# The last sample's tail: halves in another order on TensorE, two roots ahead of an output on GpSimd, two GELUs ahead of a norm on ScalarE

## The chip, the cores and the metric

One core of a Trainium2 chip runs the whole program in one launch. Its engines are TensorE (PE, matmuls; its weight loads are listed apart as PEld), VectorE (DVE), ScalarE (ACT), GpSimd (POOL) and SyncE (SP, which issues the DMAs). Each runs its own list of instructions in the order in which it is written and waits on semaphores. The metric is the device time of one launch in microseconds, the median of several runs.

## The reference

Four stages are applied to eight samples of 512 tokens with 256 features, all in float32. Only the last three touch the change.

```python
x = x + (ctx @ Wo + bo)                              # attention block
x = x + gelu2((ln(x) * g2 + beta2) @ W1 + b1) @ W2 + b2    # feed-forward "network"
# adapter 1 (domain expert), then rotation, then adapter 3 (the same with other weights):
hidden = gelu(x @ down_W.T + down_b)                 # 256 -> 64, exact GELU
hidden = hidden @ expert_W[idx].T + expert_b[idx] + domain_emb[idx]
x = hidden @ up_W.T + up_b + x                       # 64 -> 256, and the residual
x = (x - mu) * rsqrt(var + 1e-5) * ln_gamma + ln_beta
# rotation: pairs of features are turned by the sample's angles (theta, phi)
out = stack([x0*ct + x1*st, -x0*st + x1*ct, ...])
```

## The kernel before

The program has an attention part (to about 730 us) and a network part. In the network part a loop over samples j is software-pipelined: while sample j goes through the feed-forward network, sample j-1 is in adapter 1 (l = 0) and sample j-2 in adapter 3 (l = 1). Data lie mostly with features on the 128 partitions, as two feature halves c = 0, 1 (DC = 2) of 512 tokens. A layer norm needs tokens on the partitions, so TensorE transposes into PSUM banks, VectorE takes statistics, and GpSimd computes (variance + eps) ** -0.5, called a root here (`inverse_root`, `near_inverse_root`, `last_root`).

The loop ends before the last sample. The rest is written out by hand, engine by engine, for samples w = 5, y = 6 and z = 7 (the names `near_...` belong to sample 6, `end_...` and `last_...` to sample 7). The order of these calls at the end of each engine's block is the whole schedule: there is no planner. Sample 7 is cut in two token halves h = 0, 1 of 256 tokens (two tiles t of 128 each), so that engines overlap. Its steps, each with its line in the profile:

- `last_network` (DVE L1927) adds residual and bias to the second layer's result, once for each c and h, and counts `end_x2_done` in the order (h0,c0), (h1,c0), (h0,c1), (h1,c1).
- `last_down(l, h)` (PE L1630) multiplies by the down weights, summing over c; `last_hidden(l, h)` (ACT L2118) is the GELU on it.
- `last_residual(l, h)` (PE L1645) transposes the residual into PSUM by a matmul with the identity; `last_up(l, h)` (PE L1653) adds the up product on top.
- `last_statistics` (DVE L1948, L1934, L1936: statistics, aggregation, and variance + eps into `end_std`), `last_root` (POOL L2226), `last_normalise` (DVE L1954).
- `last_features` (PE L1664) transposes back, `last_features_out` (ACT L2124) copies to SBUF as `end_feat`, and `last_turned` (DVE L1962 tensor_scalar twice, then L1966 scalar_tensor_tensor twice) applies the rotation into `end_x4`.
- The same again with l = 1, and then `last_scale` (L1972) and `last_output` (L1980) on DVE, and two stores by SP (L1388).

Beside these steps the engines still finish samples 5 and 6. ScalarE normalises both (`normalise_w` L2131, `near_normalise` L2139), and GpSimd multiplies by gamma and adds beta for both: `output(w)` is `scale` (L2194) and `shift` (L2200), and sample 6 has `near_scale` (L2237) and `near_output` (L2243). Each of these four is one TENSOR_TENSOR of 128x1024 that reads and writes SBUF. `keep_busy` (L261) issues matmuls whose result nobody reads. `link` on DVE marks an instruction and waits for it, where the next one needs its result.

Of the kernel before, what the change touches and what calls it, by code (L numbers as in the profile page):

```python
# [1208 lines left out]
def network_block(nc, d, v, k, x1_dram):  # L1209
# [10 lines left out]
    with ExitStack() as ctx:  # L1220
# [3 lines left out]
        def sem(name):  # L1224
            return ctx.enter_context(nc.semaphore(name))
# [30 lines left out]
        def wait(eng, signal, j, n):  # L1256

            value = signal.at(j, n)
            if value > 0:
                eng.wait_ge(signal.sem, value)  # L1260
# [45 lines left out]
        end_res = x3[:, 0].rearrange("p c (u d) -> p (c u) d", d=D)  # L1306
        end_stats, end_mv = sb("end_stats", [P, 2, QT, 6]), sb("end_mv", [P, 2, QT, 2])
        end_std, end_rstd = sb("end_std", [P, 2, QT]), sb("end_rstd", [P, 2, QT])
        end_down, end_gelu, end_up0, end_up1, end_shifted, end_root, end_norm = (sem("end_" + n) for n in (
            "down", "gelu", "up0", "up1", "shifted", "root", "norm"))  # L1310
        end_x2_done, end_back, end_feats, end_x4_done, end_out, end_stored, end_step = (sem("end_" + n) for n in (
            "x2", "back", "feats", "x4", "out", "stored", "step"))
        END_A, END_B = (2, 0), (3, 1)
# [1 line left out]
        def end_tile(l, n):  # L1315

            h, t = divmod(n, ET)
            return bank[END_B[h]][:, t * D:(t + 1) * D] if l == 0 else bank[4 + n][:, 0:D]

        def cols(h):  # L1320

            return slice(h * EH, (h + 1) * EH)
# [71 lines left out]
        def _(pe):  # L1394
# [226 lines left out]
                        if t == QT - 1:  # L1621
                            last.then_inc(to_t[2].sem, 1)

            def last_down(l, h):
                for c in range(DC):
                    if l == 0:
                        pe.wait_ge(end_x2_done, 2 * c + h + 1)
                    elif c == 0:
                        pe.wait_ge(end_feats, DC * (h + 1))
                    last = pe.matmul(bank[END_A[h]][HALVES[l], 0:EH], k["down_w"][:, 0, c] if l == 0 else end_down_w[:, c],  # L1630
                                     (end_x2, end_feat)[l][:, c, cols(h)], start=(c == 0), stop=(c == DC - 1), tile_position=(0, A * l))
                last.then_inc(end_down, 1)

            def last_residual(l, h):

                if l == 0:
                    pe.wait_ge(end_x2_done, 2 * DC if h else DC + 1)
                elif h == 1:
                    wait(pe, norm_done[2], y, 1)
                for c in range(DC):  # L1640
                    if l == 1:
                        pe.wait_ge(end_x4_done, DC * h + c + 1)
                    for t in range(ET):
                        tok = h * EH + t * P
                        pe.matmul(end_tile(l, ET * h + t)[:, c * P:(c + 1) * P], (end_x2, end_x4)[l][:, c, tok:tok + P], ident[:],  # L1645
                                  start=(c == 0 and (l == 1 or t == 0)), stop=False, is_transpose=True, skip_group_check=True)

            def last_up(l, h):
                pe.wait_ge(end_gelu, nth(l, h))
# [45 lines left out]
            up_of_two()  # L1695
            for q in range(4, 8):
                second_layer(z, q)
            last_down(0, 0)
            last_residual(0, 0)
            last_down(0, 1)  # L1700
            last_up(0, 0)
            last_residual(0, 1)
            last_up(0, 1)
            wait(pe, norm_done[2], w, 1)
            keep_busy(pe, bank[5], w2h[:, 0], 4)
            last_features(0)
            last_features(1)
            last_down(1, 0)
            last_residual(1, 0)
            last_down(1, 1)  # L1710
            last_up(1, 0)
            last_residual(1, 1)
            last_up(1, 1)

        @block.vector
        def _(dve):
# [154 lines left out]
            def link(ins):  # L1871

                steps[0] += 1
                ins.then_inc(end_step, 1)
                dve.wait_ge(end_step, steps[0])
# [82 lines left out]
            def last_turned(h):  # L1958

                dve.wait_ge(end_feats, DC * (h + 1))  # L1960
                for c in range(DC):
                    last = dve.tensor_scalar(end_scaled[:, c, cols(h)], end_feat[:, c, cols(h)], turn[:, 0, c, z:z + 1],  # L1962
                                             turn_b[:, c, z:z + 1], ALU.mult, ALU.add)
                link(last)
                for c in range(DC):
                    dve.scalar_tensor_tensor(end_x4[:, c, cols(h)], end_feat[:, 1 - c, cols(h)], turn[:, 1, c, z:z + 1],  # L1966
                                             end_scaled[:, c, cols(h)], ALU.mult, ALU.add).then_inc(end_x4_done, 1)

# [54 lines left out]
        def _(act):  # L2023
# [91 lines left out]
            def last_hidden(l, h):  # L2115
                act.wait_ge(end_down, nth(l, h))
                rows = HALVES[l]
                act.activation(end_hid[rows, cols(h)], bank[END_A[h]][rows, 0:EH], ACT.Gelu, bias=end_down_b[rows, 0:1]  # L2118
                               ).then_inc(end_gelu, 1)

            def last_features_out(h):
                act.wait_ge(end_back, h + 1)
                for c in range(DC):
                    act.copy(end_feat[:, c, cols(h)], bank[END_A[h]][:, c * EH:(c + 1) * EH]).then_inc(end_feats, 1)  # L2124

            def normalise_w():

                act.wait_ge(near_shift, 1)
                wait(act, scaled, w - 1, 1)
                for t in range(QT):  # L2130
                    last = act.activation(features(xh[:, 2, t], 2), halves(bank[4 + t // 2][:, (t % 2) * D:(t % 2 + 1) * D]), ACT.Identity,  # L2131
                                          bias=std[:, 2, t:t + 1], scale=rstd[:, 2, t:t + 1])
                last.then_inc(norm_done[2].sem, 1)

            def near_normalise():

                act.wait_ge(near_shift, 2)
                for t in range(QT):
# [17 lines left out]
            gelu(z, 7)  # L2156
            hidden_of_two()
            normalise_w()
            near_normalise()
            last_hidden(0, 0)  # L2160
            last_hidden(0, 1)
            last_features_out(0)
            last_features_out(1)
            last_hidden(1, 0)
            last_hidden(1, 1)

        @block.gpsimd
        def _(pool):
# [84 lines left out]
            output(w - 1)  # L2253
            inverse_root(w, 2)
            near_inverse_root(1)
            output(w)
            near_scale()
            last_root(0, 0)
            last_root(0, 1)
            near_output()  # L2260
            last_root(1, 0)
            last_root(1, 1)
# [92 lines left out]
```

## Time and profile before

| | us |
|---|---|
| median of 3 runs | 1001.78 (1001.27 to 1002.12) |
| the profiled execution, as device time | 1005.43 |
| its span in the trace | 1003.6 |
| PE / DVE / ACT / POOL busy in it | 941.1 / 753.2 / 689.6 / 699.7 |
| mean granted TensorE clock | 0.986 of full speed |
| core's engines from 979 to 1003.6: PE / DVE / ACT / POOL busy | 14.72 / 15.46 / 5.74 / 12.25 of 24.60 |

The profiled execution is 3.65 us longer than the median run, and 1.8 us of it lie outside the span. Nearly all of the program is bound by TensorE (941.1 of 1003.6 us), but the change touches only what comes after the last sample's second layer, from about 979 us on. There TensorE is busy for 60% of the time and the engines wait for one another. So the views to read are the chain that ended last, and the timeline of each engine over the last 25 us. In a timeline, instructions of one line that follow one another are merged: x4 with 1.90 us are four of them, and a start plus the time is the end of the last. An instruction's time includes what it waited for after it was started, for instance for the way to memory; the idle time in brackets comes before the start.

### The profile page before, as it was taken

To read this page: it belongs to the slowest core of one execution; us is meant where nothing else is said; L and a number is where in the kernel's file an instruction comes from. 1 tells how busy PE (TensorE), PEld (TensorE's weight loads), DVE (VectorE), ACT (ScalarE), POOL (GpSimd) and SP (SyncE) were. 2 spreads that over 40 slices of the span, in tenths; PEclk is the share of its full clock that TensorE was granted. 3 is DMA by queue.
4 is the path that set the end of the run, shared out by engine and by line. 5 is a ranking of instruction groups with operands and counts; after the bars stand their busy time and mean duration, and the time that the engine had idled before them with its cause. 6 is when DMAs were issued, how large, how long until landed. Compare 5 with 4: busy or idle time off the path is not lost. (4 is left out here: it accounts for less than half of the span.)

```text
span 1003.6 us, 20024 instructions
## 1 busy us (share of the span) xinstructions
PE 941.1 (94%) x5838; PEld 619.2 (62%) x5838; DVE 753.2 (75%) x2002; ACT 689.6 (69%) x1124; POOL 699.7 (70%) x540
## 2 busy tenths in 40 slices
PE   5879999999998999999999899989999999999996
PEld 4646656655655665665565566555477777777573
DVE  7787878789869787887878888788444765668466
ACT  3377888798788789778879787978644444444332
POOL 2468788788869778877876987876554545557465
PEclk9889999999999999999999999999999999999998
DMA  8977996996897799599689879966111110111101
GB/s 271 300 294 265 371 359 229 342 389 239 297 389 284 278 361 357 196 335 384 237 292 372 333 242 342 372 250 232 64 64 43 42 43 22 42 64 42 43 22 63
DMA packets 127533, 229.96 MB, mean 229 GB/s; under 512 B 6512, under 2 KB 53872, under 8 KB 123632
## 3 DMA queue, kind: packets, MB, share of 16 engines
q1 hardware_dynamic: 127472, 229.26, 63.0%
q8 instruction: 25, 0.41, 0.2%
q14 instruction: 36, 0.29, 0.1%
HBM read 187.30 MB, written 41.94 MB: 228 GB/s over the span
## 5 line engine op out<-in xcount | busy, mean ns | idle before, releaser
L935 ACT ACTIVATE prob<-prob,nmax 128x512 f32<-128x512 f32 x512 | 356.9, 729 | 60.5 <-DVE nmax L760 57.7
L760 DVE CUSTOM_DVE_ANT_0 prob<-s_bank,big 128x512 f32<-128x512 f32 x512 | 339.4, 686 | 70.1 <-POOL big L1099 31.2
L1099 POOL TENSOR_TENSOR big<-big,mterm_early 128x2048 f32<-128x2048 f32 (+2 forms) x88 | 305.2, 3484 | 72.4 <-DMA big<-in_fside_Bx16xSxS 63.0
L591 PEld LDWEIGHTS t_bank<-ident,prob 128*128 128x128 f32 x2048 | 239.8, 141 | 167.9 <-issue 53.5
L591 PE MATMUL t_bank<-ident,prob 128*128 128x128 f32 x2048 | 318.4, 278 | 15.6 <-ACT prob L935 6.7
L942 ACT COPY pt<-t_bank 128x512 f32<-128x512 f32 x312 | 181.4, 584 | 58.0 <-PE t_bank L591 56.4
L579 PE MATMUL s_bank<-stack_k,stack_q 128*128 128x512 bf16 x512 | 196.5, 384 | 1.9 <-DVE nmax L760 1.6
L769 DVE COPY pt<-t_bank 128x512 f32<-128x512 f32 x200 | 137.5, 688 | 40.9 <-PE t_bank L591 40.6
L605 PE MATMUL o_bank<-pt,val 128*32 128x512 f32 x1024 | 122.9, 598 | 1.2 <-ACT pt L942 0.7
L2173 POOL TENSOR_TENSOR gl<-big,gh 128x512 fp32r<-128x512 f32 x64 | 83.1, 1306 | 49.4 <-DVE gh L1723 49.4
L2032 ACT ACTIVATE big<-bank,late 128x512 f32<-128x512 f32 x62 | 42.7, 690 | 72.6 <-PE bank L1438 69.0
L1099 POOL TENSOR_TENSOR big<-big,mterm_late 128x1024 f32<-128x1024 f32 (+1 forms) x16 | 50.0, 3123 | 31.7 <-DMA big<-in_fside_Bx16xSxS 31.7
L579 PEld LDWEIGHTS s_bank<-stack_k,stack_q 128*128 128x128 bf16 x512 | 50.2, 98 | 25.9 <-DVE nmax L760 12.5
L605 PEld LDWEIGHTS o_bank<-pt,val 128*32 128x32 f32 x1024 | 26.9, 109 | 59.4 <-issue 55.7
L2178 POOL TENSOR_TENSOR xtl<-xt,xth 128x512 fp32r<-128x512 f32 x14 | 17.7, 1281 | 58.0 <-ACT xt L2058 58.0
L581 PE MATMUL s_bank<-mterm_early,ident_bf 128*128 128x512 bf16 x152 | 58.0, 382 | 0.0
L1786 DVE SCALAR_TENSOR_TENSOR big<-bank,up_b,x 128x512 f32<-128x512 f32 x22 | 15.5, 745 | 53.8 <-PE bank L1512 53.8
L635 PE MATMUL spare<-xth,w_parts 128*128 128x512 f32 x128 | 52.5, 428 | 0.7 <-DVE xtl L807 0.7
L1438 PE MATMUL bank<-xth,w1h 128*128 128x512 f32 x124 | 51.6, 416 | 1.7 <-PEq L289 1.0
L1456 PE MATMUL bank<-gh,w2h 128*128 128x512 f32 x128 | 52.3, 409 | 0.0
L1456 PE MATMUL bank<-gh,w2l 128*128 128x512 f32 x128 | 50.2, 392 | 0.0
L1723 DVE CAST gh<-big 128x512 fp32r<-128x512 f32 x64 | 38.3, 610 | 14.6 <-ACT big L2032 14.3
(245 smaller groups left out, 1464.9 us busy)
## 6 DMA issues: line engine op xcount, KB each, us to landing
big<-in_fside_Bx16xSxS SPq DMA_DIRECT2D x128, 1024.0 KB, 8.0
pieces_dram<-pieces SPq DMA_DIRECT2D x64, 384.0 KB, 7.2
stack_q<-pieces_dram SPq DMA_DIRECT2D x15, 1024.0 KB, 8.1
stack_k<-pieces_dram SPq DMA_DIRECT2D x15, 1024.0 KB, 9.4
pieces_dram<-pieces SPq DMA_DIRECT2D x32, 256.0 KB, 7.4
xin<-in_x SPq DMA_DIRECT2D x8, 512.0 KB, 8.8
x_dram<-x SPq DMA_DIRECT2D x8, 512.0 KB, 2.6
x1r<-x_dram SPq DMA_DIRECT2D x8, 512.0 KB, 4.4
```

Source lines behind the costliest of these rows:

```text
L579: last = pe.matmul(bank, stack_q[:, h, t * P:(t + 1) * P], stack_k[:, h, :], start=True, stop=not by_pe)
L581: last = pe.matmul(bank, ident_bf[:], mterm[:, t, :], start=False, stop=True)
L591: last = pe.transpose(t_bank[n % 2][:, c * P:(c + 1) * P], prob[:, n % NT, c * P:(c + 1) * P], ident[:])
L605: last = pe.matmul(o_bank[VW * j:VW * (j + 1), :], val[:, c, G * g + j, :], pt[:, pt_slot(G * g + j), c, :], start=(c == 0), stop=(c == QT ...
L635: last = pe.matmul(spare[n % 2][:, :], wx[name][:, part, i * P:(i + 1) * P], x[:, part, :], start=(part == m == 0), stop=(part == 1 and m ...
L760: dve.tensor_tensor_reduce(out=prob[:, n % NT, :], in0=s_bank[n % 3][:, :], in1=bias[:, h % NB, t, :], scale=-1.0, scalar=3e38, op0=ALU.ad ...
L769: dve.tensor_copy(pt[:, pt_slot(h), :, t * P:(t + 1) * P], t_bank[n % 2][:, :].rearrange("p (c q) -> p c q", c=QT)).then_inc(evac[1].sem, 1)
L935: act.activation(tile, tile, ACT.Exp, bias=nmax[:, n % NT:n % NT + 1], scale=-1.0).then_inc(exped.sem, 1)
L942: act.copy(pt[:, pt_slot(h), :, t * P:(t + 1) * P], t_bank[n % 2][:, :].rearrange("p (c q) -> p c q", c=QT)).then_inc(evac[0].sem, 1)
L1099: pool.tensor_tensor(bias[:, h % NB, tiles], bias[:, h % NB, tiles], mterm[:, tiles], ALU.add).then_inc(masked.sem, 1)
L1456: last = pe.matmul(bank[c][:, :], w[:, f, c * P:(c + 1) * P], gx[:, f, :], start=(m == 0), stop=(m == len(parts) - 1))
L2173: pool.tensor_tensor(gl[:, f], g[:, f % NGT], gh[:, f], ALU.subtract).then_inc(gl_done.sem, 1)
```

## The change

On TensorE, `last_down` and `last_residual` are cut by feature half c. For l = 0 the parts with c = 0 now come ahead of those with c = 1. For l = 1 the two down products of a half stay together and the residual follows. The discarded matmuls of `keep_busy` ahead of `last_features(0)` go from 4 to 6, and 3 more stand between `last_features(0)` and `last_features(1)`. On ScalarE the two GELUs of sample 7's adapter 1 come ahead of sample 6's norm, and a new step `last_scaled(h)` makes one of the two products of the rotation (c = 1) that VectorE made before. On GpSimd, sample 5's `scale` is followed by sample 7's first two roots, and then by `shift` and `near_scale`.

```diff
-            def last_down(l, h):
-                for c in range(DC):
-                    if l == 0:
-                        pe.wait_ge(end_x2_done, 2 * c + h + 1)
-                    elif c == 0:
-                        pe.wait_ge(end_feats, DC * (h + 1))
...
-            def last_residual(l, h):
-
+            def last_down(l, h, c):
                 if l == 0:
-                    pe.wait_ge(end_x2_done, 2 * DC if h else DC + 1)
-                elif h == 1:
-                    wait(pe, norm_done[2], y, 1)
...
+                    pe.wait_ge(end_x2_done, 2 * c + h + 1)
+                elif c == 0:
+                    pe.wait_ge(end_feats, DC * (h + 1))
...
+            def last_residual(l, h, c):
+
+                if l == 0:
+                    pe.wait_ge(end_x2_done, 2 * c + h + 1 if h == 0 else 2 * DC)
+                else:
+                    pe.wait_ge(end_x4_done, DC * h + c + 1)
+                    if h == 1:
+                        wait(pe, norm_done[2], y, 1)
...
-            last_down(0, 0)
-            last_residual(0, 0)
-            last_down(0, 1)
+            last_down(0, 0, 0)
+            last_residual(0, 0, 0)
+            last_down(0, 1, 0)
+            last_down(0, 0, 1)
+            last_down(0, 1, 1)
+            last_residual(0, 0, 1)
             last_up(0, 0)
-            last_residual(0, 1)
+            last_residual(0, 1, 0)
+            last_residual(0, 1, 1)
             last_up(0, 1)
             wait(pe, norm_done[2], w, 1)
-            keep_busy(pe, bank[5], w2h[:, 0], 4)
+            keep_busy(pe, bank[5], w2h[:, 0], 6)
             last_features(0)
+            keep_busy(pe, bank[5], w2h[:, 0], 3)
             last_features(1)
...
             def last_turned(h):
                 dve.wait_ge(end_feats, DC * (h + 1))
-                for c in range(DC):
-                    last = dve.tensor_scalar(end_scaled[:, c, cols(h)], end_feat[:, c, cols(h)], turn[:, 0, c, z:z + 1],
-                                             turn_b[:, c, z:z + 1], ALU.mult, ALU.add)
-                link(last)
+                link(dve.tensor_scalar(end_scaled[:, 0, cols(h)], end_feat[:, 0, cols(h)], turn[:, 0, 0, z:z + 1],
+                                       turn_b[:, 0, z:z + 1], ALU.mult, ALU.add))
                 for c in range(DC):
+                    if c == 1:
+                        dve.wait_ge(end_scaled_done, h + 1)
                     dve.scalar_tensor_tensor(end_x4[:, c, cols(h)], end_feat[:, 1 - c, cols(h)], turn[:, 1, c, z:z + 1],
                                              end_scaled[:, c, cols(h)], ALU.mult, ALU.add).then_inc(end_x4_done, 1)
...
+            def last_scaled(h):
+                act.wait_ge(end_feats, DC * (h + 1))
+                act.activation(end_scaled[:, 1, cols(h)], end_feat[:, 1, cols(h)], ACT.Identity, bias=turn_b[:, 1, z:z + 1],
+                               scale=turn[:, 0, 1, z:z + 1]).then_inc(end_scaled_done, 1)
...
             normalise_w()
-            near_normalise()
             last_hidden(0, 0)
             last_hidden(0, 1)
+            near_normalise()
             last_features_out(0)
+            last_scaled(0)
             last_features_out(1)
             last_hidden(1, 0)
+            last_scaled(1)
             last_hidden(1, 1)
...
-            output(w)
-            near_scale()
+            scale(w)
             last_root(0, 0)
             last_root(0, 1)
+            shift(w)
+            near_scale()
             near_output()
```

GpSimd's last instructions before, from sample 5's gamma product on (`res` belongs to sample 5, `xt` to sample 6, `end_rstd` are sample 7's roots):

```order
L2194 TENSOR_TENSOR res<-xh,late 128x1024 [waits stored,norm_done2]
L2200 TENSOR_TENSOR res<-res,late 128x1024 [waits scaled]
L2237 TENSOR_TENSOR xt<-xh,late 128x1024 [waits norm_done2]
L2226 TENSOR_TENSOR end_rstd<-end_std,minus_half 128x2 [waits end_shifted] x2
L2243 TENSOR_TENSOR xt<-xt,late 128x1024 [waits scaled]
L2226 TENSOR_TENSOR end_rstd<-end_std,minus_half 128x2 [waits end_shifted] x2
```

and the same place now:

```order
L2210 TENSOR_TENSOR res<-xh,late 128x1024 [waits stored,norm_done2]
L2242 TENSOR_TENSOR end_rstd<-end_std,minus_half 128x2 [waits end_shifted] x2
L2216 TENSOR_TENSOR res<-res,late 128x1024 [waits scaled]
L2253 TENSOR_TENSOR xt<-xh,late 128x1024 [waits norm_done2]
L2259 TENSOR_TENSOR xt<-xt,late 128x1024 [waits scaled]
L2242 TENSOR_TENSOR end_rstd<-end_std,minus_half 128x2 [waits end_shifted] x2
```

The first two roots have moved up past two of the 128x1024 products, and three of those now stand in one row behind them.

VectorE's rotation of sample 7 before, both token halves (`big` here is `end_feat`'s partner `end_scaled` and `end_x4`):

```order
L1962 TENSOR_SCALAR big<-big,turn,turn_b 128x256 [waits end_feats]
L1962 TENSOR_SCALAR big<-big,turn,turn_b 128x256
L1966 SCALAR_TENSOR_TENSOR big<-big,turn 128x256 [waits end_step]
L1966 SCALAR_TENSOR_TENSOR big<-big,turn 128x256
L1962 TENSOR_SCALAR big<-big,turn,turn_b 128x256 [waits end_feats]
L1962 TENSOR_SCALAR big<-big,turn,turn_b 128x256
L1966 SCALAR_TENSOR_TENSOR big<-big,turn 128x256 [waits end_step]
L1966 SCALAR_TENSOR_TENSOR big<-big,turn 128x256
```

and now:

```order
L1969 TENSOR_SCALAR big<-big,turn,turn_b 128x256 [waits end_feats]
L1974 SCALAR_TENSOR_TENSOR big<-big,turn 128x256 [waits end_step]
L1974 SCALAR_TENSOR_TENSOR big<-big,turn 128x256 [waits end_scaled]
L1969 TENSOR_SCALAR big<-big,turn,turn_b 128x256 [waits end_feats]
L1974 SCALAR_TENSOR_TENSOR big<-big,turn 128x256 [waits end_step]
L1974 SCALAR_TENSOR_TENSOR big<-big,turn 128x256 [waits end_scaled]
```

Of each half's four instructions three are left, and the third has a wait for ScalarE.

## Rows read from the trace of the kernel before

**Rows 1.** Chain that ended last: start us, us, engine, tile, line

```profile
979.96 2.38 POOL res L2194
...
984.75 2.31 POOL xt L2237
...
990.84 1.90 PE bank L1630 x4
```

**Rows 2.** GpSimd's timeline: start us, us, engine, line, operation, xcount, [idle before]

```profile
987.02 1.37 POOL L2226 TENSOR_TENSOR end_rstd<-end_std,minus_half 128x2 f32<-128x2 f32 x2
988.37 2.35 POOL L2243 TENSOR_TENSOR xt<-xt,late 128x1024 f32<-128x1024 f32 x1
...
998.61 0.86 POOL L2226 TENSOR_TENSOR end_rstd<-end_std,minus_half 128x2 f32<-128x2 f32 x1 [1.35 <-DVE end_std L1936]
```

**Rows 3.** VectorE's timeline from 983 us

```profile
983.26 0.76 DVE L1948 BATCH_NORM_STATS2 end_stats<-bank 128x6 f32<-128x256 f32 x2 [3.06 <-PE bank L1653]
...
985.98 1.10 DVE L1936 TENSOR_SCALAR end_std<-end_mv 128x2 f32<-128x2 f32 x1
987.76 1.90 DVE L1954 TENSOR_SCALAR xh<-bank,end_mv,end_rstd 128x256 f32<-128x256 f32 x4 [0.68 <-POOL end_rstd L2226]
990.28 0.92 DVE L1962 TENSOR_SCALAR big<-big,turn,turn_b 128x256 f32<-128x256 f32 x2 [0.62 <-ACT big L2124]
991.23 0.88 DVE L1966 SCALAR_TENSOR_TENSOR big<-big,turn 128x256 f32<-128x256 f32 x2
...
995.12 0.86 DVE L1948 BATCH_NORM_STATS2 end_stats<-bank 128x6 f32<-128x256 f32 x2 [1.44 <-PE bank L1653]
```

**Rows 4.** Line L1936 in the whole trace: count, ns min/median/max, first and last start

```profile
L1936 DVE TENSOR_SCALAR end_std<-end_mv x4: 169/304/1101, 984.3 to 998.4; 128x2 f32<-128x2 f32 x4
```

**Rows 5.** Stretches: us, PE, PEld, DVE, ACT, POOL busy (xcount), granted clock, DMA share, GB/s

```profile
985.50:988.80 3.30, 0.03 (x1) 0.00 (x0) 2.56 (x7) 0.00 (x0) 3.30 (x4) 1.00 0.47 159
...
989.70:992.70 3.00, 2.99 (x9) 1.51 (x9) 2.39 (x6) 1.19 (x4) 1.02 (x1) 0.50 0.35 118
```

**Rows 6.** TensorE's timeline from 979 us

```profile
979.21 1.29 PE L1630 MATMUL bank<-end_x,late 128*64 128x256 f32 x4
980.43 0.65 PE L1645 MATMUL bank<-ident,end_x 128*128 128x128 f32 x4
...
982.09 1.13 PE L1653 MATMUL bank<-uw,end_hid 64*128 64x256 f32 x4
...
984.79 0.74 PE L261 MATMUL bank<-w2h 128*128 128x256 f32 x4
988.81 0.75 PE L1664 MATMUL bank<-ident,xh 128*128 128x128 f32 x4 [3.28 <-DVE xh L1954]
...
990.77 1.97 PE L1630 MATMUL bank<-big,end_down_w 128*64 128x256 f32 x4
...
993.37 1.08 PE L1630 MATMUL bank<-big,end_down_w 128*64 128x256 f32 x4
994.38 1.13 PE L1653 MATMUL bank<-uw,end_hid 64*128 64x256 f32 x4
```

**Rows 7.** ScalarE's timeline from 979 us

```profile
979.75 1.98 ACT L2139 ACTIVATE xh<-bank,near_std,near_rstd 128x256 f32<-128x256 f32 x4
...
989.60 0.65 ACT L2124 COPY big<-bank 128x256 f32<-128x256 f32 x2 [6.99 <-PE bank L1664]
```

**Rows 8.** Line L799 from 57 to 65 us: count, ns min/median/max

```profile
L799 DVE TENSOR_SCALAR xin<-xin,mv,rstd x4: 777/779/3486, 58.8 to 63.6; 128x256 f32<-128x256 f32 x4
```

**Rows 9.** GpSimd's timeline beside Rows 8

```profile
58.03 4.07 POOL L1099 TENSOR_TENSOR big<-big,mterm_early 128x2048 f32<-128x2048 f32 x1 [2.08 <-DMA big<-in_fside_Bx16xSxS]
62.19 1.32 POOL L1085 TENSOR_SCALAR mterm_late<-mraw 128x512 bf16<-128x512 uint8 x2
```

**Rows 10.** Line L884 in the whole trace: count, ns min/median/max

```profile
L884 DVE TENSOR_TENSOR rest<-proj,pieces x2: 693/1057/1421, 25.4 to 28.7; 128x512 f32<-128x512 f32 x2
```

**Rows 11.** GpSimd's timeline beside the first of Rows 10

```profile
25.08 1.23 POOL L1154 TENSOR_SCALAR xres<-xt 128x1024 f32<-128x1024 f32 x1
```

More of the change, by code:

```diff
@@ L1308, in network_block @@
         end_std, end_rstd = sb("end_std", [P, 2, QT]), sb("end_rstd", [P, 2, QT])
-        end_down, end_gelu, end_up0, end_up1, end_shifted, end_root, end_norm = (sem("end_" + n) for n in (
-            "down", "gelu", "up0", "up1", "shifted", "root", "norm"))
+        end_down, end_gelu, end_up0, end_up1, end_shifted, end_root, end_norm, end_scaled_done = (sem("end_" + n) for n in (
+            "down", "gelu", "up0", "up1", "shifted", "root", "norm", "scaled"))
         end_x2_done, end_back, end_feats, end_x4_done, end_out, end_stored, end_step = (sem("end_" + n) for n in (
@@ L1622, in up_of_two @@
                             last.then_inc(to_t[2].sem, 1)
-            def last_down(l, h):
-                for c in range(DC):
-                    if l == 0:
-                        pe.wait_ge(end_x2_done, 2 * c + h + 1)
-                    elif c == 0:
-                        pe.wait_ge(end_feats, DC * (h + 1))
-                    last = pe.matmul(bank[END_A[h]][HALVES[l], 0:EH], k["down_w"][:, 0, c] if l == 0 else end_down_w[:, c],
-                                     (end_x2, end_feat)[l][:, c, cols(h)], start=(c == 0), stop=(c == DC - 1), tile_position=(0, A * l))
-                last.then_inc(end_down, 1)
@@ L1634, in last_residual @@
-            def last_residual(l, h):
-                if l == 0:
-                    pe.wait_ge(end_x2_done, 2 * DC if h else DC + 1)
-                elif h == 1:
-                    wait(pe, norm_done[2], y, 1)
-                for c in range(DC):
[L1641 to L1646, printed above, removed]
+            def last_down(l, h, c):
+                if l == 0:
+                    pe.wait_ge(end_x2_done, 2 * c + h + 1)
+                elif c == 0:
+                    pe.wait_ge(end_feats, DC * (h + 1))
+                last = pe.matmul(bank[END_A[h]][HALVES[l], 0:EH], k["down_w"][:, 0, c] if l == 0 else end_down_w[:, c],
+                                 (end_x2, end_feat)[l][:, c, cols(h)], start=(c == 0), stop=(c == DC - 1), tile_position=(0, A * l))
+                if c == DC - 1:
+                    last.then_inc(end_down, 1)
@@ new lines, in last_residual @@
+            def last_residual(l, h, c):
[5 more added lines that the diff above has]
+                        wait(pe, norm_done[2], y, 1)
+                for t in range(ET):
+                    tok = h * EH + t * P
+                    pe.matmul(end_tile(l, ET * h + t)[:, c * P:(c + 1) * P], (end_x2, end_x4)[l][:, c, tok:tok + P], ident[:],
+                              start=(c == 0 and (l == 1 or t == 0)), stop=False, is_transpose=True, skip_group_check=True)
@@ L1697, in _ @@
                 second_layer(z, q)
-            last_down(0, 0)
-            last_residual(0, 0)
-            last_down(0, 1)
+            last_down(0, 0, 0)
[4 more added lines that the diff above has]
+            last_residual(0, 0, 1)
             last_up(0, 0)
-            last_residual(0, 1)
+            last_residual(0, 1, 0)
+            last_residual(0, 1, 1)
             last_up(0, 1)
             wait(pe, norm_done[2], w, 1)
-            keep_busy(pe, bank[5], w2h[:, 0], 4)
+            keep_busy(pe, bank[5], w2h[:, 0], 6)
             last_features(0)
+            keep_busy(pe, bank[5], w2h[:, 0], 3)
             last_features(1)
-            last_down(1, 0)
-            last_residual(1, 0)
-            last_down(1, 1)
+            last_down(1, 0, 0)
+            last_down(1, 0, 1)
+            last_residual(1, 0, 0)
+            last_residual(1, 0, 1)
+            last_down(1, 1, 0)
+            last_down(1, 1, 1)
             last_up(1, 0)
-            last_residual(1, 1)
+            last_residual(1, 1, 0)
+            last_residual(1, 1, 1)
             last_up(1, 1)
@@ L1960, in last_turned @@
                 dve.wait_ge(end_feats, DC * (h + 1))
+                link(dve.tensor_scalar(end_scaled[:, 0, cols(h)], end_feat[:, 0, cols(h)], turn[:, 0, 0, z:z + 1],
+                                       turn_b[:, 0, z:z + 1], ALU.mult, ALU.add))
                 for c in range(DC):
-                    last = dve.tensor_scalar(end_scaled[:, c, cols(h)], end_feat[:, c, cols(h)], turn[:, 0, c, z:z + 1],
-                                             turn_b[:, c, z:z + 1], ALU.mult, ALU.add)
-                link(last)
-                for c in range(DC):
+                    if c == 1:
+                        dve.wait_ge(end_scaled_done, h + 1)
                     dve.scalar_tensor_tensor(end_x4[:, c, cols(h)], end_feat[:, 1 - c, cols(h)], turn[:, 1, c, z:z + 1],
```

## The prediction

> **What bounds the kernel now.** I read the chain that ended last first, then each engine's timeline behind 979 us, then the clock. From 980 to 988.4 us the chain lies on GpSimd: samples 5 and 6's products of 128x1024, 2.3 to 2.4 us each, run one behind the other [rows 1], and sample 7's two roots come only at 987.02, two in 1.37 us [rows 2]. VectorE is held up as well: the 128x2 instruction that prepares the second root lasts from 985.98 for 1.10 us, to the end of GpSimd's product of 984.75, where 0.17 would do [rows 1, 3, 4]. Sample 7's normalise starts at 987.76. TensorE has nothing to do meanwhile: 0.03 us of 3.30 are busy [rows 5]. It comes back at 988.81, and soon has half of its clock (0.50 from 989.70 to 992.70, its 1.2 GHz level) [rows 5, 6]. The down product of half 0 therefore takes 1.97 us and not 1.08, and is in the chain [rows 1, 6]. From the statistics at 995.12 on, VectorE works through to the end.
>
> **The change, part by part.**
>
> *TensorE's new order in front.* Up (0,0) starts 2.88 us after 979.21 [rows 6]. Two down products at 1.01 (993.37 to 994.38) and a residual of four transposes at 0.65 make 2.7, without the wait for c = 1 that there was between the two down instructions: up (0,0) starts near 981.9; I take 0.15 earlier. Its GELU must be ready: the second down part of h = 0 ends near 981.2, and the GELU takes 0.5, as one of the four norm instructions of 256 columns does (1.98 for four) [rows 7], so 981.7. Before, that GELU stood behind sample 6's norm, which ended at 981.73. So ScalarE's swap is worth nothing beyond that 0.15. ScalarE idles for a microsecond and sample 6's norm ends near 984.2; GpSimd wants it much later.
>
> *GpSimd's roots.* Both halves' statistics move forward by the same 0.15 [rows 3]; GpSimd is idle from 982.34 [rows 1], so no 128x2 instruction is held up. The first variance is there at 984.3 - 0.15 + 0.17 = 984.3, the second at 985.98 - 0.15 + 0.17 = 986.0 [rows 3, 4]. Root 0 is long done, so normalise of half 0 starts at 986.0; root 1 runs from 986.07 to 986.77 (0.69 each [rows 2]); half 1 is normalised by 987.75 (0.95 each half), not 989.66: **1.9 us gained**.
>
> *The additional idle matmuls.* 0.185 us each (4 in 0.74) [rows 6]. Six end at 985.8, so TensorE's idle time shrinks to 1.1 us and I take the full clock for the features and for down (1,0). The three between the features cost 0.3 us; VectorE, below, hides them. down (1,0) ends near 989.7.
>
> *What is now beside the rotation.* This is the dear part. GpSimd's three products come from 986.77 on, 2.35 each [rows 2]: to 989.1, 991.5 and 993.9. VectorE's rotation falls right beside them. The copies for it end 1.45 us after the transposes' start (988.81 to 989.60, and 0.65) [rows 6, 7]; the transposes start behind half 0's normalise, at 986.95, so the copies end at 988.4. Before, only its first instruction met GpSimd: the pair of L1962 took 0.92 from 990.28, with GpSimd's last product until 990.72, and the two of L1966 ran free, 0.88 [rows 2, 3].
>
> What happens when both engines have a row of such instructions? The first of four L799 takes 3.49 us, to the end of GpSimd's product, and the three behind it take 0.78 each, though nothing but GpSimd's train of L1085 stands against them: VectorE and GpSimd take turns, one instruction each [rows 8, 9]. L884, which has two inputs in SBUF as L1966 has, takes 1.42 us and not 0.69 behind a GpSimd instruction of 1.23 [rows 10, 11]. So I let every instruction of the rotation wait for one product:
>
> - tensor_scalar (h0, c0): issued at 988.4, runs when the first product ends, done at 989.2. A link follows, and GpSimd's second product is in before the next instruction.
> - scalar_tensor_tensor (h0, c0): behind the second product (which VectorE pushed back a little, to 991.5): done at 991.9.
> - scalar_tensor_tensor (h0, c1): behind the third, 991.8 to 994.15: done at **994.5**.
> - h1: 0.4, then 0.45 twice, free: done at 995.7.
>
> Before, (h0, c1) was done at 992.11 [rows 3]. ScalarE's new product (0.5 us) is ready long before and saves nothing here. TensorE now waits from 989.7 to 994.5 with 0.3 us of work in it, an idle time longer than the one that halved the clock before [rows 5]; so it comes back at half clock. Then: half a residual 0.5 (0.65 for a whole one at full clock, less overlap), down (1,1) 1.9 (1.97 less its overlap with the next), first tile of up (1,0) 0.75 (994.38 to 995.12). Statistics (1,0) start at 994.5 + 0.05 + 0.5 + 1.9 + 0.75 = 997.7 instead of 995.12. VectorE's end behind it is as before (no big product is left then, and up (1,1) keeps ahead). **Sum: +2.6 us**: 1.9 gained at the norm, 4.5 lost behind it. Made against the profiled span it gives 1006.2 (1008.0 as its device time); the median runs are 3.65 us under that, and I carry the difference over as it is: 1001.78 + 2.6 = 1004.4.
>
> Bounds of what no row shows. A scalar_tensor_tensor with two SBUF inputs beside a GpSimd product: at best unhindered, 0.44 [rows 3], at worst one product each, 2.35; I take the second, for that of L884 is nearest [rows 10]. The only hint at L1966's own kind is the root of 998.61, which took 0.86 beside L1980 and not 0.69 [rows 2]. ScalarE's Identity product of 128x256: 0.33 to 0.5 [rows 7], off the path. The stores of samples 5 and 6 are issued 4.4 and 3.5 us later, at 989 and 994.2, and have left the queue before sample 7's. TensorE's end at half clock: nothing up to 2 us, if up (1,1) falls in it as well.
>
> The Trainium skill says it too ("SBUF — State Buffer", Who interferes with whom): a VectorE instruction contends with a GpSimd instruction that reads SBUF if it has two SBUF inputs, and the loser is blocked for the whole instruction. By that rule the time is the +2.6 above; by the trace of L1966 alone [rows 3], where it met no product, it would be the second rival's. The trace agrees for tensor_tensor, 1.42 against 0.69 us [rows 10]; no row shows it for scalar_tensor_tensor held up by GpSimd.
>
> **Rivals.**
>
> 1. *The clock stays up.* The same waits, but half a residual, down (1,1) and up cost 0.3 + 1.0 + 0.74: statistics at 996.6, **+1.5 us, 1003.3**. For it: 5 more idle matmuls. Against: the long wait comes behind all of them.
> 2. *Only tensor_scalar waits.* Then the two behind it follow at once, x4 of h0 is whole at 990.2; the tensor_scalar of h1 waits for the second product (991.7), statistics (1,0) start at 992.6, the variance meets the end of the third product for nothing. 995.12 - 992.6 = **2.5 us faster, 999.3**. For it: the 0.88 of L1966. Against: L884 [rows 10]. This is the case on the other side; it decides at whether scalar_tensor_tensor is held by a product.
> 3. *VectorE keeps its turn.* Both scalar_tensor_tensor and the tensor_scalar of h1 go together between the second and third product; only the last two wait, to 995.7, where statistics begin: **+0.6 us, 1002.4**. Against: L799 [rows 8].
> 4. *No turn is lost, but the gain is*: something else, as the norm of half 1 or the stores, gives the 1.9 back. **0, 1001.8**.
>
> **How the numbers follow.** About 2.0 us, 0.2%, is what a measurement of this kernel can tell from no change. Forecast (its own range 1003.3 to 1005.4): 0.48, of it 0.40 slower by over 0.2% and 0.08 within. Rival 1: 0.12 (0.03 slower, 0.09 within). Rival 2: 0.25 (0.21 faster, 0.04 within). Rival 3: 0.10 and rival 4: 0.05, within. That makes faster 0.21, same 0.36, slower 0.43. The range of 8 in 10 has to take in most of rival 2: 999.0 to 1005.2.
>
> **What would show it.** Right: roots at about 984.4 and 986.1; normalise from 986.0; then three GpSimd products in a row with a VectorE instruction of about 2.4 us ending behind each of the second and third; TensorE's longest idle time before residual (1,0) and down (1,1), with granted clock 0.5 there; statistics (1,0) near 997.7. Wrong: L1974 at 0.48 beside a product (rival 2), or both L1974 behind one product (rival 3); the clock at 1.0 in down (1,1) (rival 1); or a first normalise not before 987, which would upset every step.

## The result, and the profile after

The changed kernel takes 1003.78 us (median of 22 runs, 1001.90 to 1008.25), the kernel before 1000.78 us (22 runs beside them). The ratio is 1.004 with a 95% interval of 1.003 to 1.005: 3 to 5 us slower, where 2.6 us were forecast, and 1003.78 is inside the forecast's own range.

The two profiled executions can't be compared by their spans (1003.6 before, 1002.5 after), since the part ahead of the change, the same program in both, took 5.5 us less in the second. So every kernel below is compared by its **tail**: from VectorE's first `last_network` instruction with c = 1 (979.32 us before, 973.84 after) to the end of its last output (1001.01, and 999.02 + 0.88 = 999.90 after). Times with a plus sign are counted from that first instruction.

| | norm starts | x4 (h0, c1) done | statistics (1,0) start | tail |
|---|---|---|---|---|
| before | +8.44 | +12.79 | +15.80 | 21.70 |
| after, forecast | +6.7 | +15.2 | +18.4 | 24.3 |
| after, measured | +6.61 | +14.93 | +18.76 | 26.06 |

The chain that ended last, in the kernel after (start us, us, engine, tile, line):

```profile
980.54 0.91 DVE xh L1962 x2
...
982.96 0.86 DVE big L1969
...
983.85 4.94 DVE big L1974 x2
...
988.83 0.69 PE bank L1644 x2
989.51 1.90 PE bank L1629 x4
991.41 2.00 PE bank L1652 x4
993.42 1.04 PE bank L1644 x4
994.46 2.02 PE bank L1652 x4
```

GpSimd is no longer in it, but VectorE's two scalar_tensor_tensor of the rotation are, with 4.94 us. GpSimd's timeline, which answers to [rows 2]:

```profile
978.98 0.70 POOL L2242 TENSOR_TENSOR end_rstd<-end_std,minus_half 128x2 f32<-128x2 f32 x1 [2.10 <-DVE end_std L1944]
980.62 0.70 POOL L2242 TENSOR_TENSOR end_rstd<-end_std,minus_half 128x2 f32<-128x2 f32 x1 [0.95 <-DVE end_std L1944]
981.29 2.38 POOL L2216 TENSOR_TENSOR res<-res,late 128x1024 f32<-128x1024 f32 x1
983.62 2.39 POOL L2253 TENSOR_TENSOR xt<-xh,late 128x1024 f32<-128x1024 f32 x1
986.09 2.40 POOL L2259 TENSOR_TENSOR xt<-xt,late 128x1024 f32<-128x1024 f32 x1
```

and VectorE's, which answers to [rows 3]:

```profile
982.96 0.85 DVE L1969 TENSOR_SCALAR big<-big,turn,turn_b 128x256 f32<-128x256 f32 x1 [0.61 <-ACT big L2132]
983.85 4.92 DVE L1974 SCALAR_TENSOR_TENSOR big<-big,turn 128x256 f32<-128x256 f32 x2
988.70 0.40 DVE L1969 TENSOR_SCALAR big<-big,turn,turn_b 128x256 f32<-128x256 f32 x1
989.13 0.88 DVE L1974 SCALAR_TENSOR_TENSOR big<-big,turn 128x256 f32<-128x256 f32 x2
992.60 0.43 DVE L1956 BATCH_NORM_STATS2 end_stats<-bank 128x6 f32<-128x256 f32 x1 [2.59 <-PE bank L1652]
```

Read the two side by side. The tensor_scalar of 982.96 ends at 983.81, when the product of 981.29 is over; two scalar_tensor_tensor take 4.92 us and end at 988.77, when the products of 983.62 and 986.09 are both over; the same two take 0.88 us in the next half, where GpSimd is idle. The waits are inside the instructions' times: no idle time stands ahead of them. The four of L1974 by themselves (count, ns min/median/max), where 477 is one that waits for nothing:

```profile
L1974 DVE SCALAR_TENSOR_TENSOR big<-big,turn x4: 477/1464/2556, 983.8 to 989.5; 128x256 f32<-128x256 f32 x4
```

TensorE's timeline, which answers to [rows 6]:

```profile
979.19 0.98 PE L261 MATMUL bank<-w2h 128*128 128x256 f32 x6
981.50 0.75 PE L1663 MATMUL bank<-ident,xh 128*128 128x128 f32 x4 [1.33 <-DVE xh L1962]
...
983.08 1.08 PE L1629 MATMUL bank<-big,end_down_w 128*64 128x256 f32 x4
986.35 0.44 PE L1644 MATMUL bank<-ident,big 128*128 128x128 f32 x2 [2.19 <-DVE big L1974]
988.83 0.69 PE L1644 MATMUL bank<-ident,big 128*128 128x128 f32 x2 [2.04 <-DVE big L1974]
989.45 1.97 PE L1629 MATMUL bank<-big,end_down_w 128*64 128x256 f32 x4
991.34 2.07 PE L1652 MATMUL bank<-uw,end_hid 64*128 64x256 f32 x4
```

and stretches of it (us, PE, PEld, DVE, ACT, POOL busy, granted clock, DMA share, GB/s), which answer to [rows 5]:

```profile
983.00:986.30 3.30, 1.16 (x6) 0.47 (x4) 3.26 (x3) 2.16 (x5) 3.22 (x3) 1.00 0.47 159
986.30:988.83 2.53, 0.44 (x3) 0.20 (x3) 2.53 (x2) 0.00 (x0) 2.19 (x1) 0.59 0.00 0
988.83:996.40 7.57, 7.57 (x18) 4.08 (x18) 3.63 (x11) 0.47 (x1) 0.71 (x1) 0.50 0.20 69
```

Down (1,0), which had half the clock before, has all of it now (1.08 us). After the two waits the clock is at 0.50, the 1.2 GHz level, for everything that TensorE still has to do: down (1,1) 1.97, both up products 2.07 each where 1.13 would do.

### The profile page after: what moved, and what is told of

The parts are those of the page before. It is cut to its first block and busy times, and to the rows that moved or that the text cites. A ratio compares the mean times of both kernels' runs of the same rounds, so it can differ in the third digit from the quotient of the medians.

```text
span 1002.5 us, 19955 instructions
## 1 busy us (share of the span) xinstructions
PE 933.0 (93%) x5763; PEld 616.2 (61%) x5843; DVE 754.7 (75%) x2000; ACT 689.9 (69%) x1126; POOL 699.9 (70%) x540
## 5 line engine op out<-in xcount | busy, mean ns | idle before, releaser
L579 PE MATMUL s_bank<-stack_k,stack_q 128*128 128x512 bf16 x432 | 165.3, 383 | 2.1 <-DVE nmax L760 1.8
```

The lines of the kernel that those rows point to most:

```text
L579: last = pe.matmul(bank, stack_q[:, h, t * P:(t + 1) * P], stack_k[:, h, :], start=True, stop=not by_pe)
```

## The experiments

Each kernel was profiled once and, but for one, timed in rounds with the kernel before, whose median was 999.67 us beside e1 to e4, 1000.53 beside e5 to e8 and 1002.45 beside e9 and e10. All tails are of the one profiled execution. The ratios are those of the record, and not quotients of the medians.

| | edit | tail | ratio to before (95%) |
|---|---|---|---|
| before | | 21.70 | |
| after | | 26.06 | 1.003 to 1.005 |
| e1 | before, with the new GpSimd order alone | 26.53 | 1.0047 to 1.0088 |
| e2 | after, without the new GpSimd order | 21.79 | 1.0003 to 1.0023 |
| e3 | after, rotation reads PSUM | 19.14 | 0.9969 to 0.9993 |
| e4 | after, idle matmuls in the waits | 23.08 | 1.0021 to 1.0049 |
| e5 | after, only scalar_tensor_tensor reads PSUM | 19.18 | 0.9957 to 0.9995 |
| e6 | after, products in quarters | 20.42 | 0.9955 to 0.9989 |
| e7 | after, one product less | 20.89 | not timed |
| e8 | e3 with three more edits | 19.61 | 0.9940 to 0.9975 |
| e9 | e3 with 14 idle matmuls | 19.13 | 0.9948 to 0.9996 |
| e10 | e8 with 14 idle matmuls, ScalarE reordered | 18.63 | 0.9950 to 0.9988 |

**e1, the new GpSimd order alone.**

```diff
-            output(w)
-            near_scale()
+            scale(w)
             last_root(0, 0)
             last_root(0, 1)
+            shift(w)
+            near_scale()
             near_output()
```

> The kernel before, with GpSimd's new order alone (scale of sample 5, sample 7's two roots, then three 128x1024 products); TensorE, ScalarE and VectorE as before. The tail is counted from VectorE's first last_network instruction with c = 1 to the end of its last output: 21.70 us in the profile of before, 26.06 of after. My theory (each VectorE instruction of the rotation waits for one product): the norm starts 1.8 us earlier, at +6.6 to +6.8, the rotation's first three instructions end behind one product each and x4 of (h0, c1) is done near +15.3, where it was +12.79; TensorE comes back at half clock; tail 25 to 26.5 us, time +3 to +4 us against before. Rival (the loss lies in TensorE's new order, the nine idle matmuls or ScalarE's work): this kernel keeps the gain of the roots and is 1.5 to 2 us faster than before, tail near 20.

Measured: a tail of 26.53 us, 1004.38 us against 999.67, ratio 1.0067 (1.0047 to 1.0088), which is more than the 3 to 4 us that I expected. The norm starts at +6.74, x4 (h0, c1) is done at +15.37. The whole loss is in this one edit. VectorE's timeline of it, with two tensor_scalar per half as before:

```profile
981.67 3.18 DVE L1962 TENSOR_SCALAR big<-big,turn,turn_b 128x256 f32<-128x256 f32 x2 [0.61 <-ACT big L2124]
984.89 2.91 DVE L1966 SCALAR_TENSOR_TENSOR big<-big,turn 128x256 f32<-128x256 f32 x2
```

The products there run from 980.00, 982.32 and 984.78. The first tensor_scalar waits for the first, the second, though no semaphore stands between the two, for the second, and the first scalar_tensor_tensor for the third: three turns in another split. The fourth instruction is free.

**e2, everything but the new GpSimd order.**

```diff
-            scale(w)
+            output(w)
+            near_scale()
             last_root(0, 0)
             last_root(0, 1)
-            shift(w)
-            near_scale()
             near_output()
```

> The changed kernel with GpSimd's order as it was before (sample 5's output, sample 6's gamma product, then sample 7's roots, then one product). My theory: all the loss is the roots' move, so this one has none of it; the norm starts at +8.3, one product meets only the first tensor_scalar of the rotation, and the six idle matmuls leave TensorE idle for 2.8 us, so the clock may or may not fall: tail 20.5 to 22 us, time -1.3 to +0.3 us against before. Rival (the loss is in the rest of the change): +3 us, tail near 25.

Measured: a tail of 21.79 us, 1000.26 us against 999.67, ratio 1.0013 (1.0003 to 1.0023), so 0.3 to 2.3 us slower, at or above the upper end of what I expected. The rival is out: the rest of the change costs at most 0.2%, and it brings nothing. The profile says why: with the norm at +8.48 TensorE is idle for 3.21 us ahead of the features, more idle matmuls or not, and down (1,0) again takes 1.97 us. ScalarE's new product also has a price that I had missed, since it stands behind a GELU that waits for that slow down product:

```profile
988.88 0.48 DVE L1974 SCALAR_TENSOR_TENSOR big<-big,turn 128x256 f32<-128x256 f32 x1 [1.39 <-ACT big L2137]
```

**e3, the rotation reads the features from PSUM.** The features lie in the PSUM bank from which ScalarE copies them, so VectorE can take them there; the down product, which would overwrite that bank, goes to another, and ScalarE's GELU reads it there (that line is left out here).

```diff
-link(dve.tensor_scalar(end_scaled[:, 0, cols(h)], end_feat[:, 0, cols(h)],
+link(dve.tensor_scalar(end_scaled[:, 0, cols(h)], bank[END_A[h]][:, 0:EH],
...
-dve.scalar_tensor_tensor(end_x4[:, c, cols(h)], end_feat[:, 1 - c, cols(h)],
+dve.scalar_tensor_tensor(end_x4[:, c, cols(h)], bank[END_A[h]][:, (1 - c) * EH:(2 - c) * EH],
...
-pe.matmul(bank[END_A[h]][HALVES[l], 0:EH],
+pe.matmul(bank[(END_A, END_B)[l][h]][HALVES[l], 0:EH],
```

> The changed kernel, with VectorE's rotation reading the features from their PSUM bank and not from SBUF (so scalar_tensor_tensor has one SBUF input, and tensor_scalar none); down (1,h) writes its product to the bank of sample 7's first norm, which is free by then. GpSimd's order stays the new one. My theory (what waits is an instruction with two SBUF inputs, or a tensor_scalar from SBUF to SBUF): the three products no longer hold the rotation, L1974's takes 0.9 us for two and not 4.92, x4 of (h0, c1) is done near +10, TensorE stays at the full clock, tail 18 to 19.5 us, time -2 to -3.5 us against before. Rival (VectorE is slowed by GpSimd's products whatever it reads, for instance by its write to SBUF): L1974 still takes 4 us or more, time +2 to +4.

Measured: a tail of 19.14 us, 996.97 us against 999.67, ratio 0.9981. Its timelines of VectorE and of GpSimd:

```profile
981.34 0.54 DVE L1969 TENSOR_SCALAR big<-bank,turn,turn_b 128x256 f32<-128x256 f32 x1 [0.61 <-ACT big L2132]
981.92 0.88 DVE L1974 SCALAR_TENSOR_TENSOR big<-bank,turn,big 128x256 f32<-128x256 f32 x2
```

```profile
979.66 2.38 POOL L2216 TENSOR_TENSOR res<-res,late 128x1024 f32<-128x1024 f32 x1
981.99 2.37 POOL L2253 TENSOR_TENSOR xt<-xh,late 128x1024 f32<-128x1024 f32 x1
```

The same three products run at the same place (the third from 984.43), and the rotation runs through them at its own speed; the tensor_scalar takes 0.54 us from PSUM where it takes 0.40 from SBUF. It is what VectorE reads that makes it wait, and not GpSimd's being busy. Without the waits the clock stays at 1.00 to the end of TensorE's work. The tail is 2.56 us shorter than before's, and 1.83 us of that are the earlier norm. No run reads from PSUM with the old GpSimd order, so what the new order alone is worth is not shown.

**e4, the clock alone.**

```diff
             last_down(1, 0, 1)
+            wait(pe, norm_done[2], y, 1)
+            keep_busy(pe, bank[7], w2h[:, 0], 11)
             last_residual(1, 0, 0)
+            keep_busy(pe, bank[7], w2h[:, 0], 12)
             last_residual(1, 0, 1)
```

> The changed kernel with idle matmuls in TensorE's two long waits: 11 ahead of residual (1,0,0) and 12 ahead of residual (1,0,1), 0.16 us each. The waits of the rotation stay as they are. My theory (the clock is a loss of its own behind the waits): x4 of (h0, c1) is done at +14.9 as in after, granted clock 1.00 in down (1,1) and both up products, statistics (1,0) at +17.0 and not +18.76, tail 22.8 to 24 us, so 2 to 3 us faster than after and 0.5 to 1.5 slower than before. Rival (the clock costs little, the statistics wait for VectorE and ScalarE anyway): within 0.5 us of after.

The wait that is added, for sample 6's norm, was over long before (at 979.17). Measured: a tail of 23.08 us, 1002.00 us against 999.67, ratio 1.0035 (1.0021 to 1.0049). VectorE's waits are the same (x4 (h0, c1) at +15.02), TensorE's timeline and clock are not:

```profile
989.94 1.08 PE L1629 MATMUL bank<-big,end_down_w 128*64 128x256 f32 x4
990.95 1.13 PE L1652 MATMUL bank<-uw,end_hid 64*128 64x256 f32 x4
```

```profile
985.00:994.00 9.00, 7.33 (x43) 5.20 (x42) 7.93 (x13) 1.39 (x3) 4.86 (x3) 1.00 0.35 118
```

So of the 4.36 us by which the tail of after is longer than before's, the half clock is 26.06 - 23.08 = 2.98 us, and the rest is 23.08 - 21.70 = 1.38 us. That rest is a difference: from the norm's start to x4 (h0, c1) e4 takes 8.41 us and before 4.35, so the waits cost 4.06 more than before; the norm gives 1.83 of it back, and 0.84 comes back between x4 and the statistics (2.17 us and not 3.01), where before's TensorE was still in its slow down (1,0).

This holds for the two profiled executions. The timed runs don't confirm its size: I expected e4 to be 0.5 to 1.5 us slower than before and 2 to 3 faster than after, and it is 2.1 to 4.9 slower than before, where after is 3 to 5 slower. The profile rules out why the rival thought that the clock costs little (the statistics start at +17.19 and not +18.76), but how much of the 2.98 us there is in a usual execution stays open.

**e5, only scalar_tensor_tensor reads PSUM.** As e3 without its first edit: tensor_scalar reads `end_feat` again.

> As e3_from_psum, but only the scalar_tensor_tensor of the rotation reads PSUM; its tensor_scalar again goes from SBUF to SBUF. This is the state that my second rival assumed, so it also tests that rival's arithmetic. My theory: the first tensor_scalar lasts to the end of the first product (0.85 us as in after), the two L1974 behind it take 0.9 together; the tensor_scalar of h1 waits for the second product and takes some 1.5 to 2 us; x4 of (h0, c1) near +10.9, tail 19 to 20 us, time -1.5 to -2.8 us against before. Rival (scalar_tensor_tensor waits for its write, or for the tensor_scalar's result, rather than for a second SBUF input): L1974 over 2 us for two, tail over 22.

Measured: a tail of 19.18 us, ratio 0.9976. VectorE:

```profile
983.03 0.85 DVE L1969 TENSOR_SCALAR big<-big,turn,turn_b 128x256 f32<-128x256 f32 x1 [0.61 <-ACT big L2132]
983.91 0.88 DVE L1974 SCALAR_TENSOR_TENSOR big<-bank,turn,big 128x256 f32<-128x256 f32 x2
984.70 1.53 DVE L1969 TENSOR_SCALAR big<-big,turn,turn_b 128x256 f32<-128x256 f32 x1
```

Each tensor_scalar waits for a product, each scalar_tensor_tensor with one input in SBUF goes free. The down product writes to the other bank here as in e3, and the tensor_scalar waits all the same, so that move is not what frees VectorE. It is the state that the second rival of the prediction took for the kernel after, and its 2.5 us under before are met in the tail (21.70 - 19.18 = 2.52), with 0.5 to 4.3 us in the times.

**e6, the products in quarters.** Each of the three products is four instructions of 128x256.

```diff
+            def quarters(dst, src, other, op, done):
+                for t in range(QT):
+                    last = pool.tensor_tensor(dst[:, t], src[:, t], other, op)
+                last.then_inc(done.sem, 1)
```

> The changed kernel with GpSimd's three products behind the roots cut in four instructions of 128x256 each; nothing else differs. My theory (a VectorE instruction waits for the one GpSimd instruction that is running, and then has its turn): each wait falls from 2.4 to at most 0.6 us, the rotation of h0 ends near +10.5 to +11.5 where it was +14.93, TensorE keeps the full clock; GpSimd's row takes 7.2 to 9 us in all. Tail 19.5 to 21.5 us, time -0.5 to -2.5 us against before. Rival (VectorE waits until GpSimd's row is done, whatever its pieces): L1974 as long as in after, tail near 26.

Measured: a tail of 20.42 us, ratio 0.9972 (0.9955 to 0.9989), though the medians, 1000.09 and 1000.53 us, differ by only 0.44. Here are VectorE's line and the first two products of GpSimd's, count and ns min/median/max:

```profile
L1974 DVE SCALAR_TENSOR_TENSOR big<-big,turn x4: 829/885/942, 986.9 to 990.1; 128x256 f32<-128x256 f32 x4
```

```profile
L2221 POOL TENSOR_TENSOR res<-res,late x4: 725/729/730, 984.0 to 986.0; 128x256 f32<-128x256 f32 x4
L2221 POOL TENSOR_TENSOR xt<-xh,late x4: 773/838/907, 986.7 to 989.2; 128x256 f32<-128x256 f32 x4
```

No wait is longer than half a microsecond now (0.94 - 0.48). VectorE waits for the one instruction that is running, and then has its turn; x4 (h0, c1) is done at +12.12, later than my +10.5 to +11.5. The clock fell in this profile, and the rotation starts at +9.50 where it starts at +9.12 in after. That explains 0.38 us of the miss; the rest is that three instructions in a row each wait nearly half a microsecond.

**e7, one product less.** Sample 6's last product (its beta) is left out, with a root of 128x4 in its place.

```diff
             near_scale()
-            near_output()
+            wait(pool, scaled, y, 1)
+            pool.tensor_tensor(near_rstd[:, 0], near_std[:, 0], minus_half[:], ALU.pow).then_inc(out_made.sem, 1)
             last_root(1, 0)
```

> The changed kernel without sample 6's last product (its beta is not added; a root of 128x4 stands in its place), so two products and not three are in the row. My theory (one turn each): the second L1974 no longer waits; the pair takes 2.4 to 3 us and not 4.92, x4 of (h0, c1) is done near +12.6 to +13.6, 1.3 to 2.3 us earlier; the clock may still fall after 983. Rival (the pair waits for GpSimd to be idle and then runs): the same time, as the row is shorter by 2.35; what tells them apart is the end of the first L1974, which stays at +12.4 by mine.

Measured: a tail of 20.89 us (its one execution took 1000.27 us). The first scalar_tensor_tensor is done at +12.44 as in after (+12.45), the second at +12.84 and not +14.93: one turn less, 2.09 us less. The pair's row:

```profile
984.89 2.84 DVE L1974 SCALAR_TENSOR_TENSOR big<-big,turn 128x256 f32<-128x256 f32 x2
```

**e8, a better version.** To e3: no idle matmuls between the features, up (1,0) ahead of down (1,1), and variance + eps of adapter 3 on ScalarE (in e3 VectorE's took 0.67 us, to the end of the third product, where 0.17 would do).

```diff
             last_features(0)
-            keep_busy(pe, bank[5], w2h[:, 0], 3)
...
+            last_up(1, 0)
             last_down(1, 1, 0)
             last_down(1, 1, 1)
-            last_up(1, 0)
...
+            def last_shift(h):
+                act.wait_ge(end_meas, h + 1)
+                tiles = slice(ET * h, ET * (h + 1))
+                act.activation(end_std[:, 1, tiles], end_mv[:, 1, tiles, 1], ACT.Identity, bias=eps[:, 0:1]).then_inc(end_shifted, 1)
```

> From e3_from_psum, three more edits for a better version: no idle matmuls between the features; sample 7's up (1,0) ahead of down (1,1) on TensorE; and variance + eps of adapter 3 computed by ScalarE (Identity with a bias) and not by VectorE, so that no 128x2 tensor_scalar waits for the third product. My theory: statistics (1,0) start at +11.6 to +12 and not +12.74, the norm's chain on VectorE is 0.2 to 0.7 shorter, tail 17.5 to 18.5 us against 19.14 in e3, time -3 to -4.5 us against before. Rival (the chain moves to GpSimd's root (1,0) behind the third product, or to ScalarE): tail 18.8 to 19.3.

Measured: 997.75 us against 1000.53, ratio 0.9958 (0.9940 to 0.9975), but the tail is 19.61 us, longer than e3's: my 17.5 to 18.5 is missed. The profiled execution, 1003.26 us, was the longest of its 12. In it TensorE has a gap of 1.33 us ahead of the features and its clock falls in down (1,0) behind them (1.00 from 986.80 to 988.40, 0.50 from 989.00 to 992.00), and x4 of (h1, c1) waited 0.60 us for ScalarE:

```profile
986.86 0.75 PE L1664 MATMUL bank<-ident,xh 128*128 128x128 f32 x4 [1.33 <-DVE xh L1966]
...
988.44 1.74 PE L1630 MATMUL bank<-big,end_down_w 128*64 128x256 f32 x4
```

**e9, the gap filled.** e3 with `keep_busy(..., 14)` for 6.

> As e3_from_psum, with 14 and not 6 idle matmuls ahead of the first features, so that TensorE's gap of 1.33 us before them is filled; the 3 between the features stay. In the profiles of after, e3, e4 and e5 the clock stayed up behind this gap, in those of e6, e7 and e8 it fell, with the same TensorE program to this point. My theory (it falls in some executions and costs about 1 us there): tail 19.1 us as in e3, no fall between the gap and down (1,1); median 0 to 0.8 us faster than e3's, which was 0.9981 of before, so 0.9970 to 0.9980. Rival (14 end too late and push the features back, or the gap never mattered): 0.9980 to 0.9990.

Measured: a tail of 19.13 us, ratio 0.9972 (0.9948 to 0.9996). The tail is e3's to 0.01 us, so 14 do no harm; whether they help, the timing can't tell (e3's interval, 0.9969 to 0.9993, overlaps). Inconclusive.

**e10, e8 with both mended.** 14 idle matmuls, and `last_scaled(1)` ahead of `last_hidden(1, 0)`.

> As e8_best, with 14 idle matmuls ahead of the first features and ScalarE's last_scaled(1) ahead of its GELU (1,0), which had made VectorE wait 0.6 us. My theory: the clock stays up, x4 of (h1, c1) is done at +12.0 and not +12.63, statistics (1,0) at +12.0 to +12.3 and not +13.15, tail 18.3 to 18.9 us, time 0.9940 to 0.9960 of before. Rival (the end is held by GpSimd's third product or by TensorE's down (1,1), now late): tail 19 us or more, 0.9955 to 0.9975.

Measured: a tail of 18.63 us, the shortest; statistics (1,0) at +12.17. The ratio is 0.9969 (0.9950 to 0.9988), above the 0.9940 to 0.9960 expected and in the rival's range, though the tail is not in the rival's; e8 and e10 can't be told apart by it. Both are faster than the kernel before and than the changed one. The edit on GpSimd that lost 3 to 5 us is in both.

## Why the prediction was right

*TensorE's order in front, and the roots.* Right to 0.1 us: the norm starts 1.83 us earlier (1.75 forecast), and its second half ends at +8.51, 1.83 earlier (1.9 forecast). What TensorE's order and ScalarE's swap bring together is at most 0.13 us: e1, which has neither, starts the norm at +6.74. No run takes the swap alone.

*Each instruction of the rotation waits for one product.* Right, and it is the cause: e1 has it without the rest of the change, e2 the rest without it, e3 and e5 take it away by what VectorE reads, e6 and e7 change it by length and by number. x4 (h0, c1) was forecast at +15.2 and is done at +14.93. The first reading of rows that mattered was [rows 8, 9], four instructions each lengthened by another GpSimd instruction; the second was [rows 10]. The Trainium skill's rule ("SBUF — State Buffer", Who interferes with whom), that two SBUF inputs are enough for VectorE to be blocked by a GpSimd instruction that reads SBUF, was shown by no row for scalar_tensor_tensor. The trace now agrees: with two inputs in SBUF 2.56 us at most beside a product and 0.48 without one, with one input in SBUF 0.48 beside the same products (e5).

*The clock.* The mechanism was right, the term was too small. I put the half clock on half a residual and down (1,1), and "TensorE's end at half clock: nothing up to 2 us" into the bounds with the value nothing. From x4 (h0, c1) to the statistics (1,0) it took 18.76 - 14.93 = 3.83 us and not 3.2, and from there to the end 26.06 - 18.76 = 7.30 and not 5.9: "up (1,1) keeps ahead" was the step that failed, since both up products took 2.07 us. With e4 the clock's whole price is 2.98 us in the profiled executions. Sized so, the tail would have been forecast at some 26, +4.4 us, which lies in the 3 to 5 us of the timed runs, as 2.6 does not.

*The number.* It came out closer than its parts. The tail moved by 4.36 us and not by 2.6. And 1004.4 was counted from a median of 1001.78 us for the kernel before (3 runs), which is 1000.78 over 22; from there the same +2.6 gives 1003.4. That 1003.78 lies so near is in part luck.

*The rivals.* Rival 1 (the clock stays up, +1.5) is what e4 built: +1.38 in the tail, though 2.1 to 4.9 in the times. The changed kernel's own clock fell. Rival 2 is e5: 2.5 faster. Rival 3 (VectorE keeps its turn) fell with e1, where two tensor_scalar with nothing between them were held by one product each. Rival 4 has nothing for it.

*What was missed altogether.* ScalarE's new product was called "ready long before". It is so only while down (1,0) is fast: in e2 VectorE waited 1.39 us for it.

## What to carry to other kernels

Before a long GpSimd instruction is moved, look at which VectorE instructions will then run beside it and what they read: here a scalar_tensor_tensor with two inputs in SBUF and a tensor_scalar from SBUF to SBUF waited for it and let the next one in behind them, so that three of them beside a row of three products waited three times. Reading one input from PSUM, where the data lie anyway, took the wait away, and cutting the products made it short. A wait on one engine may also be paid a second time on TensorE, as the clock: in the profiled execution 4.1 us of waits came with 3.0 us of half clock.

## What the runs showed of the hardware that was not expected

- The clock's fall is not settled by the program. Behind the same gap of 1.33 us (six idle matmuls, then the wait for the norm), with the same matmuls behind it, the clock stayed at 1.00 in the profiles of after, e3, e4 and e5 and fell in those of e6 and e7 (0.54 from 983.00 to 984.70 in e7). In e8, which has no idle matmuls between the features, it fell only from 988.40 on; in e1 it stayed at 1.00 through the features and down (1,0), behind a gap of 1.58 us. A tail from a single profile can thus be off by about a microsecond, by an estimate from down (1,0), which takes 1.97 us at half clock and 1.08 at full. Before's own tail has that fall in it.
- A GpSimd tensor_tensor of 128x256 takes 0.73 us, a quarter of one of 128x1024 (2.35) would be 0.59: the cut costs 0.14 us for each piece.
- GpSimd hardly pays for VectorE's turns in its row: its products take 2.38 to 2.40 us each between VectorE's in after and 2.35 to 2.38 in e3, where VectorE doesn't wait, and the third starts at +12.25 and +12.21. The waits can be read only in VectorE's times. Between the short pieces of e6 it shows a little: 0.77 to 0.91 us against 0.73.
